# A new stage order, bank share-out and fill and drain lists in a five-block, one-core kernel

## The reference

```
h = layernorm(x) * (1 + ca) + sa
two layers:  h = h + time_mix(ln(h))        # RWKV: mixes, r/k/v/g, wkv scan over time, group norm, Wo
             h = h + channel_mix(ln(h))     # sigmoid(..@cWr) * (square(relu(..@cWk)) @ cWv)
x = x + ga * ln(h)
h = layernorm(x) * (1 + cb) + sb
gate, up = q(h) @ q(w_gate).T, q(h) @ q(w_up).T          # q: FP4 quantise + dequantise in blocks of 16
x = x + gb * (q(silu(gate) * up) @ q(w_down).T)
```

## Time and profile before

| | us |
|---|---|
| median of 3 runs | 2980.02 |
| lowest and highest run | 2975.94, 2981.84 |
| the profiled execution | 2979.97 |
| its span (first to last instruction) | 2978.2 |

### The profile page before, as it was taken

How to read it: one execution, slowest core, us unless ns; L and a number is a source line. 1 busy time by engine, 2 the same in 40 slices (tenths; PEclk the granted TensorE clock), 3 DMA queues, 4 the chain that set the end, 5 groups by cost and what they waited for, 6 DMA issues and landing times.

```text
span 2978.2 us, 79496 instructions
## 1 busy us (share of the span) xinstructions
PE 2745.6 (92%) x32829; PEld 2179.4 (73%) x32829; DVE 2420.0 (81%) x5345; ACT 1494.8 (50%) x3155; POOL 1297.6 (44%) x1457
## 2 busy tenths in 40 slices
PE   4779999999999999999999999999999999999875
...
DMA packets 36838, 41.56 MB, mean 14 GB/s; under 512 B 3273, under 2 KB 35201, under 8 KB 36481
## 3 DMA queue, kind: packets, MB, share of 16 engines
...
## 4 chain that ended last, share of the span: by engine, by line
PE 58%; DVE 24%; ACT 8%; issue 7%; POOL 3%; ACTq 0%; DVEq 0%; DMA 0%; POOLq 0%
PE ps_all L1512 9%; PE ps_all L1545 8%; PE ps_all L1526 7%; PE ps_all L1327 7%; PE ps_all L1563 5%; PE ps_all L1311 3%; PE ps_all L1357 3%; PE ps_all L1430 3%; ACT mixin L941 3%; DVE ffn_work L603 3%; DVE mixin L1120 3%; DVE stats L1053 2%; DVE ffn_work L605 2%; ACT mixin L938 2%; DVE att L1170 2%
## 5 line engine op out<-in xcount | busy, mean ns | idle before, releaser
L770 POOL TENSOR_TENSOR mixin<-mixin,hT_tm 128x512 f32<-128x512 f32 x320 | 402.1, 1273 | 355.1 <-DVE mixin L1120 355.1
L1512 PE MATMUL ps_all<-chan,cwk 128*128 128x256 f32 x1536 | 385.9, 395 | 11.9 <-DVE chan L1099 9.6
L1526 PE MATMUL ps_all<-cwv,chan 128*128 128x256 f32 x1536 | 346.8, 382 | 0.4 <-issue 0.4
L1512 PEld LDWEIGHTS ps_all<-chan,cwk 128*128 128x128 f32 x1536 | 280.3, 192 | 76.0 <-issue 33.3
L911 ACT ACTIVATE chan<-ps_all 128x512 f32<-128x512 f32 x192 | 114.7, 598 | 421.5 <-PE ps_all L1512 419.5
L1526 PEld LDWEIGHTS ps_all<-cwv,chan 128*128 128x128 f32 x1536 | 288.0, 191 | 46.9 <-issue 9.9
L750 POOL TENSOR_TENSOR rstd<-var,powc 128x2 f32<-128x2 f32 x224 | 179.3, 800 | 278.7 <-DVE var L1059 278.0
L1120 DVE SCALAR_TENSOR_TENSOR mixin<-ps_all,vcol,sxrk 128x256 f32<-128x256 f32 x640 | 270.1, 475 | 23.3 <-PE ps_all L1357 13.2
L1170 DVE COPY_PREDICATED att<-masks,ps_all 128x256 f32<-128x256 uint8 x384 | 203.9, 531 | 20.4
L938 ACT ACTIVATE mixin<-ps_all,vcol 64x256 f32<-64x256 f32 x128 | 71.8, 561 | 276.5 <-PE ps_all L1311 275.7
L799 POOL TENSOR_TENSOR mixin<-mixin,bonus 128x512 f32<-128x512 f32 x64 | 83.1, 1298 | 253.2 <-ACT mixin L941 253.2
...
## 6 DMA issues: line engine op xcount, KB each, us to landing
...
```

The lines of the kernel that those rows point to most:

```text
L770: pool.tensor_tensor(m, m, hT["tm", l][:, :, :, 1:P + 1].rearrange("p k c t -> p (k c) t"), ALU.add).then_inc(ev["mixed"][b], 1)
L1512: ins = pe.matmul(bank(b, "ck", lj, "k")[:, m * TT:(m + 1) * TT], cwk[:, l, k, n:n + P], k_in[:, k, :], start=(k == 0), stop=(k == KC - 1))
L1526: ins = pe.matmul(bank(b, "cv", l, "v")[:, c * D:(c + 1) * D], relu[t // 2][:, t % 2, c * P:(c + 1) * P], cwv[:, l, t, :], start=(t == 0), ...
```

## The change

Only tables are changed: `ORDER`, `HEAD`, `TAIL` and `SECOND`. Every stage is still done once for every step, with the same instructions, tiles and shapes. The lines behind the tables are numbered two lower in the changed kernel, since the tables are two lines shorter. `HEAD_BLOCKS` and `TAIL_BLOCKS` stay 5 and 3. The new `ORDER` begins at another point of the cycle and all its lags are one smaller, so that the fill list now reaches one step further and the drain list begins one step later.

```
 ORDER = {
-    PE: """0/2 lev.3; 4/5 gu.1.0; 0/2 kt; 1/3 lev.1; 0/2 so ov; 3/4 ck.2; 4/5 gu.1.1; ...
+    PE: """3/3 ck.0; 0/1 pg; 1/2 pw1 pk pr; 0/1 lev.2; 1/2 pw2 pv; 3/3 ck.1; 0/1 lev.3; 4/4 ht.0; 0/1 kt; 4/4 gu.1.0; ...
...
-SECOND = """0 mf.2 m; 1 so t; 2 ck.2 k; 3 ck.0 k; 3 ck.1 k; 3 ck.2 k; 3 cv v; 4 dn o; 4 gu.0.0 g; 4 gu.0.1 g; 4 gu.1.0 g; 4 gu.1.1
-    u; 4 ht.0 a; 4 ht.1 b"""
+SECOND = """0 mf.2 m; 0 so t; 1 so t; 2 ck.1 k; 2 cr r; 3 ck.0 k; 3 ck.1 k; 3 cr r; 4 dn o; 4 gu.0.0 g; 4 gu.0.1 g; 4 gu.1.0 g; 4
+    gu.1.1 u; 4 ht.0 b; 4 ht.1 a; 4 xt x"""
```

More of the change, by code:

```diff
@@ L26 @@
 ORDER = {
[L27 to L38, removed]
```

298 lines of the change are left out of this document (154 added, 144 removed).

## The result

The changed kernel takes 2951.71 us (median of 4 runs, 2948.29 to 2957.65), the kernel before 2977.98 (4 runs, 2975.49 to 2981.84). The ratio is 0.9913, 95% interval 0.9898 to 0.9928. The forecast was 2990 us, the range 2962 to 3010: wrong in direction and outside the range. The profiled execution of the changed kernel took 2948.29 us, its span 2946.6.

The account below looks back on a forecast made before the run. PE was taken to bound the kernel, only just, idle 3.1 of 86.7 us a turn. +12 us from 24 turns at +0.5, drain -1.5 and fill 0 made +10 on 2979.97: 2990 us, range 2962 to 3010.

Parts of the forecast that it names:

- sum of a turn: Repeated part: PE's lost and added waits in one turn, summed to +0.5 us, for 24 turns.
- the whole first third gains nothing: First third of a turn, through turn.cm(3): waits that go, -1.1 us, are cancelled by new waits, +1.4.
- ht.0: PE would wait for DVE's qc.0, delayed 2.9 us by block 0's stages and 0.75 by ACT's order: +1.0 a turn.
- fill: First step: delays from moved weight normalisations are given back by a transpose of weights: 0, bounds -6 and +6 us.
- Turn, waits that go: PE's waits at xt, turn.tm(1), pw1(1) and lev.3(0) disappear: together -1.7 us a turn.
- so(1), ov(1): Directly behind turn.tm(0): so(1) waits for ACT to read bank 7, ov for a DVE result: +0.3 us a turn.
- mf.0(0): Directly behind mix(0), it waits for ACT's tanh: +0.6 us a turn.
- turn.cm(3): Shares bank 6 with gu.0.0, freed only after an ACT chain beginning with xt; PE arrives early and waits: +0.5 us a turn.
- kt, gu.1.0, so(0): kt does not wait; so(0), directly behind gu.1.0, waits for ACT's sigmoid and DVE's first product: +0.1 us a turn.
- turn.cm(2): Its 0.83 us wait for DVE's lnb behind wo(0) shrinks to 0.5: -0.3 us a turn.
- Drain: Last turns: the drain begins a step later, so one slower drain turn becomes a list turn: -1.5 us.
- Gain rival: qc.0 in time, ov and turn.cm(3) cost nothing: -0.6 us a turn, -14 us, 2966 us; chance 0.29.

Follow-up runs that it names:

- a_mixbank: Changed kernel with cr(2) between mix(0) and mf.0(0) on PE, mix(0) earlier on DVE and ACT, and cr(2) in bank 6 instead of 7: 2967.93 us.
- a_gu01: Changed kernel with ACT's sigmoid for gu.0.1 back ahead of sc.1(0) and pv(0): 2954.36 us.
- a_pad: Changed kernel with one extra, neutral DVE operation of about 0.68 us ahead of qc.0: 2967.52 us.
- a_burst: Changed kernel with lev.1(1) directly behind ov(0) on PE (160 small matmuls in a row), sc.1(1) ahead of gna(0) on ACT, gu.1.1's outputs swapped between banks: 3004.70 us.
- b_shift: Kernel before with 128 repeated waits added to PE's list ahead of the first turn, 64 of them in the trace: 2978.86 us, one run.
- a_oldbanks: Changed kernel's order with the kernel before's share-out of the two shared banks: 3004.37 us.
- b_newfill: Kernel before, with its banks, and only the fill (up to the sixth turn) in the new order: 2987.74 us.
- b_newdrain: Kernel before, with its banks, and only the drain (from the twenty-seventh turn) in the new order: 2984.14 us.

## Why the prediction was wrong

Two steps of the sum of a turn failed: "the whole first third gains nothing", with mf.0's +0.6 counted as a new wait (it gained 0.7 us), and ht.0's +1.0 (it did not wait). Two more things had been put at nothing or nearly so: PE's standstills, and the fill and the drain. The 23 turns took 17.5 us less where the sum had 11.5 more, the two ends 14.1 less where it had 1.5. Term by term:

- *Turn, waits that go* (-1.7): right. xt, turn.tm(1), pw1(1) and lev.3(0) have none or 0.06.
- *so(1), ov(1)* (+0.3): 0.29 and 0.14, close.
- *mf.0(0)* (+0.6): the step "it needs ACT's tanh, the wait is 0.6" is right about the wait and wrong as a term: 0.59 + 1.22 against 1.79, net 0.0. I compared idle times only. mf.2's bank was taken from so(1) and read until late by DVE's st.1(1); a_mixbank shows on the same group that a held bank costs 0.7 us of busy time. The kernel before shows the same cause in its own rows: mf.2(0) starts 0.05 us behind DVE's last read of that bank.
- *turn.cm(3)* (+0.5): 0.47, right, with the chain as described. But "the whole first third gains nothing" failed, and the sign turned here first: PE's turn.cm(3) starts 28.5 us behind turn.tm(0) instead of 29.2, so -0.7 where the sum had +0.3. The difference is the +0.6 of mf.0 above and some 0.5 us of small gaps at wo(1) and xt. A stage that needs no wait starts about 0.1 us ahead of the modelled end of the one before it, so a wait's row understates what it costs: xt's row had 0.55, its start came 0.78 earlier.
- *ht.0* (+1.0), the largest term and the one furthest off: it did not wait, its start came 0.1 later and not 1.0. I had qc.0 1.9 us too late in the turn, and PE 0.6 too late. 0.8 of the 1.9 is the 0.75 for ACT's sigmoid, counted without the 0.7 by which DVE now comes there earlier through the gain ahead of it; a_gu01 shows that it is not on the path at all. The other 1.1 us: gu.0.1 to qc.0 takes 16.7 us instead of the 14.8 of before plus 2.9, because sc.2(0) takes 0.67 instead of 1.10, cmix(3) 2.24 instead of 2.47, and small waits close. The logic stood (a_pad: each 0.6 costs 0.5), the size was a difference of two large numbers, with an error of 1. This alone did not turn the sign, for smaller delays that I had small or not at all took its place: *kt, gu.1.0, so(0)* (+0.1) came to 0.66 by their starts, cr(3) to 0.34 (0.17 of it a wait that I had not listed), pk, pr and pw2(1) to 0.28, lev.1(1) and ck.2(3) to 0.19. The rest of the turn behind turn.cm(3) grew by 0.24 us where the sum had +0.2; that this agrees is luck.
- *turn.cm(2)* (-0.3): right.
- *Not in the sum:* PE's standstills for instructions, 0.3 a turn (7.2 us in so(0) and ov(0) in nine turns), which the new order ended by parting the row of 160. a_burst and b_shift show the cause.
- *Drain* (-1.5) and *fill* (0): -9.8 and -4.3, outside the first's bounds. Of the drain's, the last three turns bring 5.4 (88.2, 89.1 and 88.8 us became 85.5, 89.0 and 86.4) and what follows the last load 4.4 (293.2 to 288.8). Both ends depend on the banks (a_oldbanks, b_newfill, b_newdrain), which I had followed through the repeated part only. What single list entries bring stays open.

The Gain rival came nearest: -0.6 a turn by "qc.0 is in time", 2966 us; less the standstills and the two ends (7.2, 4.3 and 9.8) that is 2945, and 2948.29 was measured in the profiled execution. It was right that qc.0 is in time. That the number comes so near is partly luck: it gave ov and turn.cm(3) no wait and they have one, and its 0.6 for mf.0 was none.
